# Attention and mixture-of-experts layer on one core: joint softmax sums in four column tiles, outputs two pairs later, and a new last pair

## The reference, cut to what matters

```python
def reference(L0_attn_x, w_q, w_k, w_v, w_o, Wr, W1, W2):       # x: 4 x 1024 x 128, f32
    x = L0_attn_x
    h = _layernorm(x)                                            # attention, 16 heads of 64
    q, k, v = (einsum('bsd,hdk->bhsk', h, w) for w in (w_q, w_k, w_v))
    weights = softmax(einsum('bhqk,bhmk->bhqm', q, k) / 8, axis=-1)
    z = einsum('bhqm,bhmk->bhqk', weights, v)                    # heads side by side: 1024
    x = x + (h + einsum('bse,ed->bsd', z, w_o))
    h = _layernorm(x)                                            # 8 experts, top 1, capacity 512
    probs = softmax(h @ Wr); e = argmax(probs); p = probs[e]
    rank = number of earlier tokens that chose the same expert   # over all 4096 tokens
    y = relu(h @ W1[e]) @ W2[e] * p   if rank < 512 else 0
    return x + (h + y)
```

## Time and profile before

| | us |
|---|---|
| timed runs, median (3) | 1564.29 |
| profiled execution | 1562.23 |
| its span | 1560.4 |
| PE busy in it | 1512.3 (97%) |
| POOL busy | 1189.2 (76%) |
| DVE busy | 1067.3 (68%) |
| ACT busy | 817.0 (52%) |
| mean granted clock of PE | 0.981 of full speed |

### The profile page before, as it was taken

The page is one execution under the profiler, slowest core; times in us unless marked ns, Lnnn a source line. Parts: engine busy times, 40 slices in busy tenths (PEclk is TensorE's granted clock), DMA queues, the critical chain, the costliest instruction groups (busy, mean ns, idle before and its releaser), DMA issues.

```text
span 1560.4 us, 22018 instructions
## 1 busy us (share of the span) xinstructions
PE 1512.3 (97%) x7522; PEld 880.6 (56%) x7522; DVE 1067.3 (68%) x1340; ACT 817.0 (52%) x1599; POOL 1189.2 (76%) x665
## 2 busy tenths in 40 slices
PE   7999999999999999999999999999999999999786
PEld 4455555555555555555555555555556555554575
DVE  6667776776667766776667766777677777675532
ACT  3556554555555454555555555554655646454221
POOL 3689887787787877788777777787878979879225
PEclk8999999999999999999999999999999999999698
DMA  5323434332334333322334333322334433230431
GB/s 143 76 63 85 99 93 107 95 87 58 80 86 98 85 79 75 80 61 55 77 85 99 85 85 68 83 67 53 72 84 102 106 72 94 51 73 24 144 126 36
DMA packets 114510, 128.38 MB, mean 82 GB/s; under 512 B 40490, under 2 KB 65583, under 8 KB 114400
## 3 DMA queue, kind: packets, MB, share of 16 engines
q1 hardware_dynamic: 107488, 116.62, 32.4%
q0 software_dynamic: 2560, 6.14, 1.2%
q10 hardware_dynamic: 4352, 4.23, 0.8%
HBM read 18.91 MB, written 12.65 MB: 20 GB/s over the span
## 4 chain that ended last, share of the span: by engine, by line
PE 89%; POOL 4%; DVE 3%; issue 1%; DMA 1%; ACT 1%; SPq 1%; POOLq 0%; ACTq 0%; DVEq 0%
PE ps_w L1196 28%; PE ps_w L1182 16%; PE ps_w L1183 14%; PE ps_m L1140 10%; PE ps_m L1217 4%; PE ps_m L1122 3%; PE ps_w L1209 3%; POOL acc L537 3%; PE ps_m L1113 2%; PE ps_m L1114 2%; PE ps_m L1115 2%; DVE mxw L913 1%; PE ps_m L1418 1%; PE ps_w L1418 1%; PE ps_w L1438 0%
## 5 line engine op out<-in xcount | busy, mean ns | idle before, releaser
L537 POOL TENSOR_TENSOR acc<-acc,ring 128x1024 f32<-128x1024 f32 x380 | 903.5, 2378 | 149.3 <-ACT ring L683 108.4
L913 DVE TENSOR_REDUCE mxw<-ps_m 128x1 f32<-128x1024 f32 x508 | 598.3, 1220 | 349.7 <-PE ps_m L1140 349.7
L683 ACT ACTIVATE ring<-ps_w 128x512 f32<-128x512 f32 x1024 | 543.5, 596 | 124.6 <-PE ps_w L1183 119.9
L1196 PE MATMUL ps_w<-ring,V 128*64 128x512 f32 x2048 | 470.9, 602 | 0.0
L1182 PE MATMUL ps_w<-queriesA,keysA 128*128 128x512 f32 x1024 | 430.9, 421 | 0.7 <-ACT ring L683 0.4
L1183 PE MATMUL ps_w<-queriesB,keysB 65*128 65x512 f32 x1024 | 406.6, 397 | 0.0
L1196 PEld LDWEIGHTS ps_w<-ring,V 128*64 128x64 f32 x2048 | 136.4, 137 | 268.6 <-issue 230.6
L1182 PEld LDWEIGHTS ps_w<-queriesA,keysA 128*128 128x128 f32 x1024 | 194.2, 190 | 88.3 <-issue 46.5
L537 POOL TENSOR_TENSOR acc<-ring 128x1024 f32<-128x1024 f32 x64 | 152.7, 2386 | 105.1 <-ACT ring L683 105.0
L923 DVE RECIPROCAL sums<-sums 128x128 f32<-128x128 f32 x248 | 225.6, 931 | 0.0
L1183 PEld LDWEIGHTS ps_w<-queriesB,keysB 65*128 65x128 f32 x1024 | 194.6, 190 | 34.2 <-issue 0.7
(11 more groups left out here) (155 smaller groups left out, 969.7 us busy)
## 6 DMA issues: line engine op xcount, KB each, us to landing
queriesA<-qk_high SPq DMA_DIRECT2D x248, 128.0 KB, 2.4
keysB<-qk_high SPq DMA_DIRECT2D x124, 128.0 KB, 2.3
keysA<-qk_rest SPq DMA_DIRECT2D x124, 128.0 KB, 2.4
queriesB<-qk_rest SPq DMA_DIRECT2D x124, 128.0 KB, 2.4
keysA<-qk_high SPq DMA_DIRECT2D x93, 128.0 KB, 2.3
tokens_by_slot<-blank ACTq DMA_DIRECT2D x16, 258.0 KB, 3.9
ring<-tokens_by_slot SPq DMA_DIRECT2D x8, 516.0 KB, 6.2
wst<-in_L_attn_w_q SPq DMA_DIRECT2D x32, 64.0 KB, 2.2
```

Source lines behind the costliest of these rows:

```text
L537: pool.tensor_tensor(acc[h][:, :], before, P_both(kt), ALU.add).then_inc(summed, 1)
L683: act.activation(P_tile(kt, p), ps_s[k % 3][:, :], ACT.Exp, scale=SCALE).then_inc(exp_done, 1)
L913: dve.tensor_reduce(mxw[h][:, p * HT + qt:p * HT + qt + 1], ps_v[banks][p], AX_X, ALU.max).then_inc(maxed, 1)
L1196: mm = pe.matmul(ps_z[p * DK:(p + 1) * DK, :], V[par][:, kt * P + p * DK:kt * P + (p + 1) * DK], P_tile(kt, p), start=(kt == 0), stop=(kt ...
```

## The change

Seven things are different.

1. **Joint sums.** For pairs 0 to 29 (`joint(j)`) the sums of both halves and both heads are made at once, in quarter 0 of the next pair: four matmuls 32 columns wide, in columns and PSUM partitions 0-31 (half 0, head 0), 32-63 (half 1, head 0), 64-95 and 96-127 (head 1). There is one bank, one copy by ACT and one set of four inversions for a pair. Pairs 30 and 31 keep the old form.
2. **Spreading.** z has 64 rows a head, but a sum now stands in 32. Eight DMAs a pair (`spread_sums`, SP's queue, 64 KB each) copy the inverted sums to `by_sums[h]`, 128 rows for each half.
3. **Outputs two pairs later.** z is kept in `z[j % 2][h]` and scaled in place: half 0 in quarter 3 of pair j+1, half 1 in quarter 0 of pair j+2. `project_out` and `add_out` of pair j stand in quarters 1 and 3 of pair j+2. Pair 1 has none, pair 31 has four (29 and 30, one in each quarter). `wo` has a third buffer.
4. **POOL's waits and order.** The first addition of half h of pair j waits for `sums_done` of the joint sums of pair j-1, for h = 0 too. The four scatters `"e"`, before between additions, stand together ahead of the first one. In pair 0 half 1, the subtraction `split_low_tokens` (L525 of before) stands ahead of addition 3 instead of 5.
5. **Logits in two parts.** In pairs 25, 27 and 29 four token tiles come before score blocks 3 and 4 of quarter 2, four after them.
6. **A new end.** The last pair's z is not scaled. The sums are turned (`end_turn_sums`), so that each token has its inverse as a scalar beside it; each head is projected by itself in 64 rows (`end_project`), and DVE multiplies and adds it to the residual (`end_half`), takes moments and the mean off. The centred rows are turned and give logits before the root is known; the root scales later (`end_norm`, `end_shift`). Half 0 is done so within quarter 3, half 1 behind it. PE sums two tiles itself, POOL five.
7. **Experts.** `down(6)` comes before `up` of expert 7, and DVE's `finish(5)` and `finish(6)` with it.

The diff, cut to its core:

```diff
-        LAST_BY_PE = 4
...
+        def joint(j):
+            return j < LAST - 1
+        def sums_no(j, h):
+            return j + 1 if joint(j) else 2 * j + h + 1 - (LAST - 1)
+        def outputs(j, oct):
+            if known(j, LAST):
+                return (LAST - 2 + oct % 2, oct // 2)
+            return (j - 2, oct // 2) if j >= 2 and oct in (1, 3) else None
+        def out_no(j, h):
+            return 2 * j + h + 1 if j < LAST - 2 else 2 * (LAST - 2) + 2 * h + j - (LAST - 2) + 1
...
+            def spread_sums(j):
+                sp.wait_ge(recip_done, 4 * sums_no(j, 1))
+                for h in range(2):
+                    if j > 0:
+                        sp.wait_ge(z_ready, 2 * (j - 1) + h + 1)
+                    for p in range(2):
+                        made = sums[p * DK + h * DK // 2:p * DK + (h + 1) * DK // 2, :]
+                        for k in range(2):
+                            sp.dma_start(by_sums[h][p * DK + k * DK // 2:p * DK + (k + 1) * DK // 2, :], made
+                                         ).then_inc(spread[h], 16)
...
                     if not (j == 0):
-                        pool.wait_ge(sums_done, 2 * j + h - 1)
+                        pool.wait_ge(sums_done, sums_no(j - 1, h))
...
-                        if j in SPLIT_IN and kt == 5:
+                        if j in SPLIT_IN and kt == (3 if known(j, 0) and h == 1 else 5):
                             split_low_tokens(SPLIT_IN[j], h)
...
-                        if routed(j, "e") is not None and h == 0 and kt % 2 == 1:
-                            scatter(routed(j, "e"), [4 + kt // 2])
+                        if routed(j, "e") is not None and (h, kt) == (0, 1):
+                            scatter(routed(j, "e"), range(4, QT))
...
+                if j >= 2:
+                    act.wait_ge(wo_done, out_no(j - 2, h))
+                act.activation(z[j % 2][h][:, :], ps_z[:, :], ACT.Copy).then_inc(z_copied, 1)
...
+            def scale_z(j, h):
+                if joint(j):
+                    dve.wait_ge(spread[h], 64 * (j + 1))
                 else:
-                    dve.wait_ge(sums_copied, 2 * j + h + 1)
-                    dve.reciprocal(sums[:, c], sums[:, c]).then_inc(recip_done, 1)
-            def scale_z(j, h):
-                dve.wait_ge(recip_done, 4 * (2 * j + h) + 4)
+                    dve.wait_ge(recip_done, 4 * sums_no(j, h))
                 dve.wait_ge(z_copied, 2 * j + h + 1)
+                by = by_sums[h] if joint(j) else sums
+                dve.tensor_tensor(z[j % 2][h][:, :], by[:, :], z[j % 2][h][:, :], ALU.mult).then_inc(z_ready, 1)
...
+            def end_half(h):
+                n, b = 2 * B - 1, B - 1
+                dve.wait_ge(sums_turned, h + 1)
+                dve.wait_ge(row_numbers, B)
+                turned = end_sums[h].rearrange("p (t k c) -> p t k c", t=HT, k=2)[:, :, :, 0]
+                dve.reciprocal(end_scale[:, h, :, :], turned).then_inc(end_inverse, 1)
+                dve.wait_ge(end_inverse, h + 1)
...
+                for k in range(2):
+                    tiles = range(h * HT + 2 * k, h * HT + 2 * k + 2)
+                    dve.wait_ge(end_out, HT if h == 0 else tiles[-1] + 1)
+                    for t in tiles:
+                        c = slice((t - h * HT) * P, (t - h * HT + 1) * P)
+                        ins = dve.scalar_tensor_tensor(out=x_tile(t), in0=end_heads[h][k][0][:, c],
+                                                       scalar=end_scale[:, h, t - h * HT, 0:1], in1=x_tile(t),
+                                                       op0=ALU.mult, op1=ALU.add)
...
+                    for t in tiles:
+                        c = slice((t - h * HT) * P, (t - h * HT + 1) * P)
+                        dve.scalar_tensor_tensor(out=x_tile(t), in0=end_heads[h][k][1][:, c],
+                                                 scalar=end_scale[:, h, t - h * HT, 1:2], in1=x_tile(t),
+                                                 op0=ALU.mult, op1=ALU.add).then_inc(end_added, 1)
+                    for t in tiles:
+                        dve.wait_ge(end_added, t + 1)
+                        ins = dve.bn_stats(moment_parts[:, t, :], x_tile(t))
+                    then(ins)
...
+                    if oct == 0 and j >= 2:
+                        scale_z(j - 2, 1)
+                    if oct == (0 if last else 3) and not first:
                         scale_z(j - 1, 0)
-                    if oct == 2 and not first:
+                    if oct == 2 and last:
                         scale_z(j - 1, 1)
                     if oct == 1 and not first:
                         recip(j - 1, 1, 0)
-                    if oct == 3:
+                    if oct == 3 and known(j, LAST - 1):
                         recip(j, 0, 0)
...
+            end_root(0)
+            end_root_done(0)
+            choose(B - 1, lent_out)
+            end_shift(B - 1)
             add_totals(B - 1)
-            find_slots(B - 1, lent_turn)
+            find_slots(B - 1, lent_out)
             find_shares(B - 1)
-            choose(B, lent_qk)
-            find_slots(B, lent_qk)
+            end_half(1)
+            end_root(1)
+            choose(B, lent_out)
+            end_root_done(1)
+            end_shift(B)
+            find_slots(B, lent_out)
             find_shares(B)
...
-                    if c == 0 and e >= 2:
+                    if c == 0 and 2 <= e < E - 1:
                         finish(e - 2)
+                    if c == 0 and e == E - 1:
+                        finish(E - 2)
                 if e + 1 < E:
                     low_tokens(e + 1)
-            finish(E - 2)
+                if e == E - 2:
+                    finish(E - 3)
             finish(E - 1)
...
+                pe.wait_ge(summed, 7 * (2 * j + h) + 7 - by_pe)
+                if joint(j):
                     for p in range(2):
-                        pe.matmul(bank[p * DK:(p + 1) * DK, :], ones[:, :], P_tile(kt, p),
-                                  start=(kt == KT - by_pe), stop=False)
-                pe.wait_ge(summed, 7 * (2 * j + h) + 7 - by_pe)
+                        for half in range(2):
+                            at = p * DK + half * DK // 2
+                            mm = pe.matmul(bank[at:at + DK // 2, :], ones[:, 0:DK // 2],
+                                           acc[half][:, p * HALF:(p + 1) * HALF], start=True, stop=True)
+                    mm.then_inc(sums_done, 1)
+                    return
...
                 pe.wait_ge(z_ready, 2 * j + h + 1)
+                if known(j, LAST - 2, LAST - 1) and (j, h) != (LAST - 2, 0):
+                    pe.wait_ge(wo_added, out_no(j, h) - 1)
...
+                for i in tiles:
+                    for p in range(2):
+                        r = slice(p * DK, (p + 1) * DK)
+                        mm = pe.matmul(end_heads[h][i // 2][p][:, i * P:(i + 1) * P], z[LAST % 2][h][r, i * P:(i + 1) * P], wo[LAST % 3][r, :],
+                                       start=True, stop=True)
+                    mm.then_inc(end_out, 1)
+            def end_turn(h, k):
+                pe.wait_ge(end_centred, h * HT + 2 * k + 2)
+                if h == 1 and k == 0:
+                    pe.wait_ge(end_copied, 1)
+                for i in range(2):
+                    mm = pe.transpose(end_turns[k][:, i * P:(i + 1) * P],
+                                      rows[(B - 1) % 2][:, h * HT + 2 * k + i, 0:D], ident[:, :])
+                mm.then_inc(end_turned, 1)
...
+                    if last and oct == 3:
+                        end_turn_sums(0)
+                        end_project(0, range(HT))
+                    if c is not None and oct == 2:
+                        pe.wait_ge(maxed, all_out - 1)
+                        make_logits(c, lent_turn, range(0, HT))
...
                     if last and oct == 3:
-                        project_out(LAST, 1, 0, lent_max)
+                        end_turn(0, 0)
+                        end_turn(0, 1)
                     values(j, par, oct)
                     if oct == 0 and not first:
                         softmax_sums(j - 1, 1)
-                    if oct == 2:
+                    if oct == 2 and not joint(j):
                         softmax_sums(j, 0)
...
+            pe.wait_ge(wo_added, 2 * LAST)
+            make_logits(B - 1, lent_out, range(HT))
+            sums_by_pe(LAST, 1, LAST_BY_PE)
+            count_ranks(B - 1, lent_out)
             softmax_sums(LAST, 1, LAST_BY_PE)
...
-            turn_h2(B - 1, 0)
-            project_last(0)
-            make_logits(B - 1, lent_turn)
-            for quarter in range(1, 4):
-                project_last(quarter)
-            pe.wait_ge(last_added, 3)
-            turn_h2(B - 1, 1)
-            count_ranks(B - 1, lent_turn)
-            make_logits(B, lent_qk)
-            count_ranks(B, lent_qk)
+            pe.wait_ge(end_copied, 2)
+            end_project(1, range(2))
+            end_turn_sums(1)
```

(9 more changed lines are left out.)

270 lines of the change are left out of this document (154 added, 116 removed).

## The result

The changed kernel takes 1547.32 us (median of 4 runs, 1542.72 to 1548.15), the kernel before 1563.53 beside it: ratio 0.990, interval 0.987 to 0.992. It is faster by 16.2 us; forecast were 33.5 (1530.0), with 1519 as the low and 1546 as the high end. The profiled execution took 1542.72 us, 19.5 less than that of before, where 34.3 had been summed up. One of the later executions of this kernel (in the run after_again) took 1667.8 us at a mean granted clock of 0.842; no ratio includes it.

What follows compares the result with a forecast made beforehand. PE's instruction stream (busy 97%) was taken as the bound. Terms 22.8 + 2 + 9 + 1.5 - 1 = 34.3 us off the profiled 1562.23 gave 1527.9, and with 2.06 for the median 1530.0; range 1519 to 1546.

Steps and rivals of the forecast that it cites:

- the table: Forecast and measured gains by stage, summing to 34.3 and 19.4 us; T is the last quarter's first score block.
- GpSimd's new wait: Half 0's additions wait for the previous pair's joint sums: slack 6.4 us, cost 1 us for pairs 2 and 28 (0 to 3).
- Joint sums, TensorE: Sums in each of 30 pairs: four tiles together cost 0.98 us instead of 1.74, saving 0.76 a pair, 22.8 us.
- two at a time: Rival in the joint sums: only two tiles run together, the term becomes -3.0 us and the time 1556; chance 9%.
- in order: Rival in the joint sums: records start strictly in order, five steps, 2.27 us, 4.4 us slower, 1568.7; chance 3%.
- DVE loses four inversions a pair ... neither bounds PE, so nothing: Joint sums on other engines: DVE loses four inversions a pair and ACT one copy; counted as no gain.
- Scaling stands in quarter 3 ... Cost nothing: Scaling of z after the spread, in quarter 3: eight DMAs have 15.6 us, so no cost.
- The start: Joint sums of pair 0 start near 88.6 instead of 91.42; gain 0 to 2.7 us, taken as 0.
- Logits: Pairs 27 and 29: in two parts, drops to clock 0.50, each worth about 1.6, may go; 2 us (0 to 3.2).
- The end: Behind T: second scatters from T+28.5 instead of T+39.0, gain 10.5 less 1.5 for POOL; 9 us (5 to 12).
- Experts: `finish(5)` follows `down(5)`, so POOL's last 12 output scatters begin about 1.6 us earlier: 1.5 us (0 to 2).
- POOL late or new waits: Rival: slower additions delay joint sums, or new waits in pairs 30, 31, 1, 2 with clock drops eat 15 us: 1545; 8%.

Runs made afterwards that it cites:

- after_again: A later run of the changed kernel unchanged, as the yardstick for edited kernels; such yardstick runs measured 1546.14 and 1544.15 us.
- scale_late: Changed kernel with both z scalings of pair j-2 at the end of VectorE's quarter 0 of pair j: 1535.63 us, ratio to before 0.984.
- roots_late: Changed kernel with GpSimd's inverse roots in pairs 0 to 2 two additions later: 1534.35 us; again on another chip 1535.23 us.
- both_and_end: Changed kernel with scalings and inverse roots moved, and the end's mean subtractions given a second input in PSUM: 1532.82 us; again on another chip 1528.41.
- the yardsticks: The changed kernel run without an edit beside edited kernels, in two groups: 1546.14 us and 1544.15 us, each ratio 0.990 to the kernel before.
- all three changed kernels that were run together on one chip: Changed kernel with scalings and roots moved (1535.06 us), that plus PSUM-input end subtractions (1532.82), and changed kernel with logits in one block at the second place (1552.75).
- the fourth kernel of that group: The kernel before with its z scalings moved behind the second pair of maxima of VectorE's quarters 0 and 2: 1565.15 us, ratio 1.000.

## Why the prediction was wrong

The direction was right, and the bound (TensorE's stream) too. The size was 2.1 times too large (1.8 times by the profiled executions). By the table 14.9 us are missing: 3.5 in pairs 1 to 3, 5.0 in pairs 3 to 24, 3.0 in pairs 30 and 31 and 4.2 behind T, less 0.8 that came better than forecast. Two terms failed: the moved scalings, put at nothing, and GpSimd's new wait, put at 1 us. Step by step:

- **Joint sums, TensorE: right.** 0.99 us for the block instead of 0.98, a gain of 0.70 a pair instead of 0.76, 21 us of the 22.8. Both rivals of the tiles (two at a time, in order) are out. The Trainium skill's factor of 3.07, which it gives for four row tiles ("TensorE: Matmul & The Clock Gate", Part 3) and by which 1.12 us had been estimated, is not what these four column tiles show: eight records take two steps.
- **"DVE loses four inversions a pair ... neither bounds PE, so nothing" and "Scaling stands in quarter 3 ... Cost nothing": this is the step that failed first.** I took the scaling at its old 0.68 us wherever it stood and looked for its inputs' times, not for who else uses SBUF then. It became 1.8 to 2.2 us, VectorE had no slack in quarter 2, and TensorE's visit came 0.2 us late in 17 of 22 middle pairs: about 3.4 of the 5.0 us missing there (1.3 is the 0.06 a pair). scale_late, which moves nothing but the scalings, brings 4.6 of the 5.0 back. The 3.0 us of pairs 30 and 31 are the same step: one scaling of 3.60 us and the drop of the clock there.
- **GpSimd's new wait, "1 us for pairs 2 and 28 together (0 to 3)": the second step that failed.** I sized the slack of a middle pair (right: none of them waits) and counted scatters in pairs 2 and 28 (28 has no wait), but left out that GpSimd waits for moments in pairs 0 to 2 (7.5, 1.6 and 3.3 us); there the later start of half 0 had no reserve. It cost 3.5 us against the table's forecast, drops of the clock included. roots_late gained more than that, 9.2 us by spans, because it also removed the wait of 3.2 us in pair 1 and its drop, which the forecast of the start had taken for given.
- **The start: right in number** (sums at 88.48, forecast 88.6), in part by luck. My row put the end of GpSimd's last addition at 89.2, and I went on with 88.6; it ended at 88.43. That wait was not a fixed price either: without it the sums came at 85.37.
- **Logits: right in size (3.1 us in the two pairs, forecast 2), not in cause.** In the first place one block of 16 does as well as two of eight, so splitting was not needed; whether it would have been enough at the old place is open.
- **The end, forecast 9 us net with 1.5 for GpSimd's lateness: measured 1.7** (behind T 6.2 instead of 10.5, ahead of it 4.5 lost instead of 1.5). Ahead: the scaling of 3.60 us and its drop of the clock. Behind: 1.7 us from the held subtractions and 1.7 from the clock that fell behind them; the other 0.9 is not traced to a cause. both_and_end takes the first of these two away and not the second.
- **Experts: right,** 1.6 us from the first transpose of tokens to the end (73.6 to 72.0), forecast 1.5.
- The median lies 4.6 us above the profiled execution instead of 2.1, because that execution was the fastest of four. The other three ran at a mean granted clock of 0.980 to 0.982 against its 0.985, so they spent more time at half the clock; in which places isn't recorded.

The rival "POOL late or new waits" (1545, 8%) was the one that came true, with waits and drops of the clock in three of the pairs it names (1, 2 and 30). That its number fits as well as it does is partly luck: 5.0 of the missing 14.9 us lie in the middle pairs, where it had none, and the held instructions of VectorE it doesn't name.

Open: what delays the updates of semaphores by 3 us in the experts' stage on one chip, why a wait of one length is followed by a drop of the clock in one profile and not in another, and where in the kernel the slower executions of the yardsticks (1541 to 1549 us, mean granted clock 0.986 to 0.981) had their drops.

## What to carry to other kernels

An instruction that is moved does not keep its duration: where VectorE reads two tiles of SBUF, or copies within it, look in the trace at what GpSimd is doing at the new time, and put it into GpSimd's pauses or give it an input in PSUM. When a wait is added to one engine, check the slack not in the middle of the kernel but in the pairs with extra work, and ask what that engine could do while it waits. Look for the long ones among many executions of one instruction in the trace that you start from; the median hides them. A wait of TensorE of 2 to 3 us was often, but not always, followed by 3.4 us at half the clock, which costs 1.7 us more.

## What the runs showed of the hardware

- Four matmuls on tiles of 32 columns, two records each, run as two steps: starts 6 ns apart, 0.99 us with the change of tile width.
- VectorE with both inputs in SBUF (128x512) ended 0.55 us behind the end of GpSimd's running addition, a `tensor_scalar` from SBUF to SBUF (128x128) 0.1 us behind it; with one input in PSUM the same work was not held (0.61 us beside an addition). GpSimd's addition took 0.3 to 0.4 us longer where VectorE got in between two of them (2.65 and 2.79 us instead of 2.38). A scatter seems to hold VectorE as well: operations that began during one (1383.77; in scale_late 1388.25) ended 0.56 us behind the addition that came after it.
- Updates of the semaphore by which TensorE releases the relus in the experts' stage arrived 3 us late in one place, in all three changed kernels that were run together on one chip, and 0.3 to 0.4 us late in the fourth kernel of that group; in the ten other profiles none of this semaphore was over 0.01 us late.
